# Four graph layers on one core: h rows gathered between the rounds of message sums, the update network's first weight moved into the messages, softplus in one VectorE operation

## The reference

```python
x = _layernorm(x + L0(x, edges, edge_attr_128))     # softmax-weighted messages, 128->256->128 network
x = _layernorm(x + L1(x, edges))                    # sum of neighbours, two matmuls, batch norm, relu
x = _layernorm(x + L2(x, edges, edge_attr_20, edge_weight))
x = _layernorm(x + L3(x, edges))                    # two rounds of mean aggregation
...
# L2: W = filter network of edge_attr_20, times edge_weight; h = x @ W_in2f
# y[n] = sum over edges e with src[e] == n of h[dst[e]] * W[e]
        out = shifted_softplus(y @ W_o1 + b_o1) @ W_o2 + b_o2
```

## Time and profile before

| | |
|---|---|
| three runs | 2384.61, 2387.68, 2387.77 us (median 2387.68) |
| the profiled execution | 2379.15 us, its span 2377.4 us |
| PE busy | 2065.5 us (87%) |
| DVE busy | 1998.6 us (84%) |
| ACT busy | 1792.7 us (75%) |
| POOL busy | 1510.3 us (64%) |
| DMA | mean 182 GB/s |
| mean granted TensorE clock | 0.952 of full speed |

### The profile page before, as it was taken

The page is one execution under the profiler, slowest core; times in us unless marked ns, Lnnn a source line. Parts: engine busy times, 40 slices in busy tenths (PEclk is TensorE's granted clock), DMA queues, the critical chain, the costliest instruction groups (busy, mean ns, idle before and its releaser), DMA issues. The chain is left out here.

```text
span 2377.4 us, 45798 instructions
## 1 busy us (share of the span) xinstructions
PE 2065.5 (87%) x14016; PEld 1722.5 (72%) x14016; DVE 1998.6 (84%) x2960; ACT 1792.7 (75%) x3691; POOL 1510.3 (64%) x1115
## 2 busy tenths in 40 slices
PE   5999999999998899997998788884899995777774
PEld 4999999999997577775776677773666663666663
DVE  7999999999997566666998799993888885788886
ACT  4889899988997577776776688884899994555563
POOL 6888866777730544433555564677888874888774
PEclk9999999999999899998999899997999998789897
DMA  4767666556665888887885687884576764998763
GB/s 111 159 158 161 157 171 169 164 160 192 190 183 180 213 253 252 255 254 176 215 202 127 150 186 179 193 195 124 151 198 186 200 185 118 198 220 215 195 189 113
DMA packets 326072, 433.55 MB, mean 182 GB/s; under 512 B 114207, under 2 KB 170113, under 8 KB 325832
## 3 DMA queue, kind: packets, MB, share of 16 engines
q1 hardware_dynamic: 213528, 373.35, 56.0%
q0 software_dynamic: 112000, 56.93, 14.1%
q10 hardware_dynamic: 304, 0.36, 0.1%
HBM read 242.31 MB, written 188.97 MB: 181 GB/s over the span
## 5 line engine op out<-in xcount | busy, mean ns | idle before, releaser
L1785 POOL DMA_INDIRECT acc<-combined,first_ x100 | 211.4, 2114 | 172.0 <-DMA acc<-combined,first_ 115.8
L511 PE MATMUL banks<-mats,g_hT 128*125 128x256 f32 x1000 | 259.3, 382 | 0.0
L530 PE MATMUL banks<-mats,g_zT 128*125 128x128 f32 x2000 | 238.8, 273 | 0.0
L845 POOL DMA_INDIRECT gin_xs<-x,from_ x100 | 127.9, 1279 | 158.1 <-DMA x_of_src<-gin_xs 134.1
L530 PEld LDWEIGHTS banks<-mats,g_zT 128*125 128x125 f32 x2000 | 228.2, 188 | 0.0
L511 PEld LDWEIGHTS banks<-mats,g_hT 128*125 128x125 f32 x1000 | 189.8, 190 | 28.4 <-issue 0.4
L1013 DVE TENSOR_TENSOR gin_acc<-gin_acc,gin_qr 125x512 f32<-125x512 f32 x125 | 86.6, 693 | 116.5 <-ACT gin_qr L975 116.5
L591 ACT ACTIVATE g_zT<-banks,cols 128x500 f32<-128x500 f32 x250 | 179.1, 776 | 2.6 <-PE banks L519 2.6
L574 ACT ACTIVATE g_sq<-banks 125x512 f32<-125x512 f32 x250 | 144.8, 590 | 43.4 <-PE banks L511 43.0
L438 POOL DMA_INDIRECT g_xd<-in_x,idx x100 | 124.8, 1248 | 70.6 <-PE banks L545 43.7
L2305 POOL DMA_INDIRECT out<-el_h,to_d x100 | 130.8, 1308 | 60.7 <-issue 32.5
(11 more groups left out here) (412 smaller groups left out, 6599.1 us busy)
## 6 DMA issues: line engine op xcount, KB each, us to landing
acc<-g_zero SPq DMA_DIRECT2D x126, 224.0 KB
x<-g_x SPq DMA_DIRECT2D x125, 224.0 KB
g_x<-in_xT SPq DMA_DIRECT2D x100, 250.0 KB
gin_x<-x SPq DMA_DIRECT2D x50, 448.0 KB
h<-gin_hr SPq DMA_DIRECT2D x50, 448.0 KB
al_h<-h SPq DMA_DIRECT2D x32, 448.0 KB
al_x<-x SPq DMA_DIRECT2D x32, 448.0 KB
out<-al_out SPq DMA_DIRECT2D x32, 448.0 KB
```

Source lines behind the costliest of these rows:

```text
L511: m = nc.tensor.matmul(bank[0:P, 256 * j:256 * j + 256], HT[q % 2][:, c:c + P], K.W1c, start=False, stop=j == 1)
L530: m = nc.tensor.matmul(pO[q % 2][0:P, D * j:D * j + D], ZT[q % 2][:, h, P * j:P * j + P], K.W2[:, h, :], start=False, stop=j == R - 1 and ...
L1785: pool.indirect_dma_start(out=K.acc, out_offset=bass.IndirectOffsetOnAxis(ap=K.first[:, g, r:r + 1], axis=0), in_=CR[:, g, r * D:r * D + D ...
```

## The change

Four edits:

1. **h rows.** POOL no longer gathers h rows at the start of the messages and in `edges_middle`. Instead `get_h(k)` follows each of the 25 rounds of sums, in both stages. Tile k of the h rows goes into the tile of `combined` whose sum has just landed (tile 0 into a spare one).
2. **y rows.** Eight tiles (SPARE) are gathered at the end of `side` instead of 20, into spare tiles and tile 0 of `combined`. The other 17 are gathered in `edges_middle`, `get(k)` taking tile k + 8 once tile k of h has been turned. `put` is four tiles late instead of five.
3. **W_o1 in the messages.** `turn_m` multiplies by W_o1 instead of the identity. Since the sum over edges and the multiplication by W_o1 can be exchanged, `acc` holds y @ W_o1, and `first`, `first_d`, `copy_y`, `copy_yd` leave `edges_middle`. ACT and DVE now read the turned y in PSUM directly (pG for the source side, pT for the destination side).
4. **Softplus.** max(v, -b) + ln(1 + exp(-|v + b|)) in one `scalar_tensor_tensor`. The missing constant b - log 2 passes through W_o2 into `bias_u`. For that `Fold` gets three more small DVE operations on constants, one more matmul and one more addition, and `split_rows` (eight DVE operations in iterations 4 to 8 of the messages) makes `bias_u`. `Deferred` no longer makes it in the first layer.

The lists of `steps` for ACT and DVE in `edges_middle` are written in a new order (not shown), the last part of PE's too.

```diff
-YEARLY = 20
+SPARE = 8
...
-        elif n in (4, 5):
-            wide = (K.bias_s if n == 4 else K.bias_u)[:, :].rearrange("p (r d) -> p r d", r=R)
-            part = [p[:, D * (n - 4):D * (n - 3)].rearrange("p (o d) -> p o d", o=1).to_broadcast([128, R, D]) for p in part]
+        elif n == 4:
+            wide = K.bias_s[:, :].rearrange("p (r d) -> p r d", r=R)
+            part = [p[:, 0:D].rearrange("p (o d) -> p o d", o=1).to_broadcast([128, R, D]) for p in part]
...
+        link(nc.vector.tensor_scalar(c[8], K.c("bo1"), LOG2, None, ALU.subtract))
+        link(nc.vector.tensor_scalar(self.passed[:, :], K.ident[:, :], 0.0, c[8], ALU.mult, ALU.add))
+        link(nc.vector.tensor_scalar(c[9], K.c("bo1"), -1.0, None, ALU.mult))
+        dve.wait_ge(self.pc, 2)
         link(nc.vector.tensor_tensor(K.alone[:, :], self.pa[:, 0:128], K.bo2_rows[:, :], ALU.add))
+        link(nc.vector.tensor_tensor(self.rows[:, :], self.pa[:, 128:256], K.bo2_rows[:, :], ALU.add))
...
+    def split_rows(self, dve, n):
+        nc, K, rows, rest, part = self.nc, self.K, self.rows, self.rest, self.part
+
+        def link(ins, count):
+            ins.then_inc(self.split, 1)
+            dve.wait_ge(self.split, count)
+
+        if n == 0:
+            link(nc.vector.tensor_copy(part[0][:, :], rows[:, :]), 1)
+            link(nc.vector.tensor_tensor(rest[:, :], rows[:, :], part[0][:, :], ALU.subtract), 2)
+            link(nc.vector.tensor_copy(part[1][:, :], rest[:, :]), 3)
+        elif n == 1:
+            link(nc.vector.tensor_tensor(rows[:, :], rest[:, :], part[1][:, :], ALU.subtract), 4)
+            link(nc.vector.tensor_copy(part[2][:, :], rows[:, :]), 5)
+        elif n in (2, 3, 4):
+            wide = K.bias_u[:, :].rearrange("p (r d) -> p r d", r=R)
+            piece = part[n - 2][:, :].rearrange("p (o d) -> p o d", o=1).to_broadcast([128, R, D])
+            if n == 2:
+                link(nc.vector.tensor_scalar(wide, piece, K.ident[:, 0:1], None, ALU.mult), 6)
+            else:
+                link(nc.vector.scalar_tensor_tensor(out=wide, in0=piece, scalar=K.ident[:, n - 2:n - 1], in1=wide, op0=ALU.mult,
+                                                    op1=ALU.add), n + 4)
...
+        pe.wait_ge(self.made, 14)
+        nc.tensor.matmul(self.pa[:, 128:256], self.passed[:, :], K.W("o2"), start=True, stop=True).then_inc(self.pc, 1)
...
-                for k in range(4):
-                    ins.get(pool, k)
                 for k in range(rounds):
                     past(pool, cr, k)
                     past(pool, fi, k)
                     past(pool, added, k - 1, 16 * R)
                     sum_round(pool, K, CR, last - k, added)
+                    ins.get_h(pool, k)
                 past(pool, added, rounds - 1, 16 * R)
...
                 def turn_m(k):
                     if k == 0:
-                        pe.wait_ge(bn.made, 13)
+                        pe.wait_ge(bn.made, 17)
                     past(pe, mt, k)
                     past(pe, mr, k - 1)
                     for j in range(R):
-                        m = nc.tensor.transpose(pM[0:P, D * j:D * j + D], MT[k % 2][:, P * j:P * j + P], K.ident[:, :])
+                        m = nc.tensor.matmul(pM[0:P, D * j:D * j + D], MT[k % 2][:, P * j:P * j + P], K.W("o1"), start=True, stop=True)
...
-                steps(EG, [(1, only_last), (2, indices_of), (1, apply), (1, select), (1, weights), (0, residual), (1, sums),
+                steps(EG, [(1, only_last), (2, indices_of), (4, lambda k: bn.split_rows(dve, k)), (1, apply), (1, select), (1, weights), (0, residual), (1, sums),
...
     def side(pool):
         for i, k in enumerate(range(rounds, EG)):
             past(pool, added, i - 1, 16 * R)
             sum_round(pool, K, CR, EG - 1 - k, added)
+            ins.get_h(pool, k)
         past(pool, added, EG - rounds - 1, 16 * R)
-        for m in range(YEARLY):
-            ins.get_y(pool, m, got)
-        pool.wait_ge(got, 16 * R * YEARLY)
+        for m in range(SPARE):
+            ins.get_y(pool, m)
+        pool.wait_ge(ins.h_got, 16 * R * EG)
+        for m in range(SPARE):
+            pool.wait_ge(ins.y_got[m], 16 * R)
...
+    def sums(self, g):
+        return self.CR[:, g, :].rearrange("p (r d) -> p r d", r=R)
+
+    def H(self, k):
+
+        return self.spare[0] if k == 0 else self.sums(EG - k)
+
+    def Y(self, m):
+
+        if m >= SPARE:
+            return self.H(m - SPARE)
+        return self.spare[m + 1] if m + 1 < SPARE else self.sums(0)
...
                 def get(k):
-                    if k >= 4:
-                        past(pool, hT, k - 4)
-                        ins.get(pool, k)
+                    if k + SPARE < EG:
+                        past(pool, hT, k)
+                        ins.get_y(pool, k + SPARE)
...
-                for k in range(YEARLY, EG):
-                    ins.get_y(pool, k, ins.y_late[k - YEARLY])
-                steps(EG, [(0, get), (5, put)])
+                steps(EG, [(0, get), (4, put)])
...
-                steps(EG, [(0, load), (0, load_d), (2, keep_h), (2, keep_x3d), (2, keep_hd)])
+                steps(EG, [(0, load), (0, load_d), (2, keep_h), (2, keep_x3d), (3, keep_hd)])
...
-                    past_slot(pe, got, k, 16 * R)
-                    past(pe, ydt, k - 1)
+                    past(pe, spd, k - 1)
...
                 def turn_y(k):
-                    past(pe, bt, k)
-                    if k >= YEARLY:
-                        pe.wait_ge(ins.y_late[k - YEARLY], 16 * R)
+                    past(pe, sp_, k - 1)
+                    pe.wait_ge(ins.y_got[k], 16 * R)
                     for j in range(R):
-                        m = nc.tensor.transpose(pT[:, P * j:P * j + P], ins.Y(k)[:, j, :], K.ident[0:P, 0:P])
+                        m = nc.tensor.transpose(pG[:, P * j:P * j + P], ins.Y(k)[:, j, :], K.ident[0:P, 0:P])
                     m.then_inc(yT, 1)
 
                 def turn_yd(k):
                     past_slot(pe, din, k, 80)
-                    past(pe, yt, k)
+                    past(pe, bt, k)
...
-                def first(k):
-                    past(pe, yt, k)
-                    past(pe, rld, k - 1)
-                    past(pe, abd, k - 1)
-                    nc.tensor.matmul(pG[:, 0:G], K.W("o1"), YT[k % 2][:, :], start=True, stop=True).then_inc(o1, 1)
-
-                def first_d(k):
-                    past(pe, ydt, k)
-                    past(pe, rl, k)
-                    past(pe, ab, k)
-                    nc.tensor.matmul(pG[:, 0:G], K.W("o1"), YTD[k % 2][:, :], start=True, stop=True).then_inc(o1d, 1)
...
-                steps(EG, [(0, turn), (0, turn_y), (0, turn_back), (1, turn_x3), (0, first), (0, turn_yd), (1, hidden), (1, turn_x3d),
-                           (0, first_d), (1, back_h), (1, second), (0, update), (1, hidden_d), (0, update_d), (1, back_hd)])
+                steps(EG, [(0, turn), (0, turn_y), (2, back_hd), (1, turn_x3), (0, turn_back), (0, turn_yd), (1, hidden), (1, turn_x3d),
+                           (0, update), (1, second), (1, back_h), (1, hidden_d), (0, update_d)])
...
-                def copy_y(k):
+                def size(k):
                     past(act, yT, k)
-                    past(act, o1, k - 2)
-                    nc.scalar.activation(YT[k % 2][:, :], pT[:, 0:G], ACT.Copy).then_inc(yt, 1)
-
-                def copy_yd(k):
-                    past(act, ydT, k)
-                    past(act, o1d, k - 2)
-                    nc.scalar.activation(YTD[k % 2][:, :], pT[:, 0:G], ACT.Copy).then_inc(ydt, 1)
-
-                def size(k):
-                    past(act, o1, k)
...
-                def positive(k):
-                    past(dve, ab, k)
+                def soft(k):
+                    past(dve, l1, k)
                     past(dve, upd, k - 2)
-                    nc.vector.tensor_scalar(SP[k % 2][:, :], pG[:, 0:G], K.c("bo1"), 0.0, ALU.add, ALU.max).then_inc(rl, 1)
-
-                def soft(k):
-                    past(dve, rl, k)
-                    past(dve, l1, k)
-                    nc.vector.scalar_tensor_tensor(out=SP[k % 2][:, :], in0=SP[k % 2][:, :], scalar=LOG2, in1=AB[k % 2][:, :],
-                                                   op0=ALU.subtract, op1=ALU.add).then_inc(sp_, 1)
-
-                def positive_d(k):
-                    past(dve, abd, k)
+                    nc.vector.scalar_tensor_tensor(out=SP[k % 2][:, :], in0=pG[:, 0:G], scalar=floor, in1=AB[k % 2][:, :],
+                                                   op0=ALU.max, op1=ALU.add).then_inc(sp_, 1)
+
+                def soft_d(k):
+                    past(dve, l1d, k)
                     past(dve, updd, k - 2)
-                    nc.vector.tensor_scalar(SPD[k % 2][:, :], pG[:, 0:G], K.c("bo1"), 0.0, ALU.add, ALU.max).then_inc(rld, 1)
-
-                def soft_d(k):
-                    past(dve, rld, k)
-                    past(dve, l1d, k)
```

(34 more changed lines are left out.)

49 lines of the change are left out of this document (23 added, 26 removed).

## The result

The change makes the kernel faster by 0.6%: the ratio is 0.9942, 95% interval 0.9927 to 0.9956, and the medians of 20 runs each are 2386.51 us before and 2374.74 us after (their own quotient, 0.9951, lies inside). Forecast were 2369.4 us and a chance of 0.74 for this side.

A forecast was written before the change was run, and what follows sets the result against it. PE was taken to bound the messages, POOL's `get_y` nodes alone; in edges middle ACT, PE, DVE and POOL were nearly full. Terms -1.9 + 10.5 - 14 - 12.9 = -18.3 from 2387.68 gave 2369.4 us, range 2350 to 2393.

The forecast's parts named there:

- First layer, -1.9: First layer: DVE loses 1.9 us of work on `bias_u`, with work queued behind it; the other bound is 0.
- Messages, +10.5 forecast: Messages: PE's added work and POOL's gathers give the same end, stage 10.5 us longer, +7 to +14.
- `split_rows`, taken as 0: Messages: its added DVE work fits into DVE's free time and PE's delay, costing 0, at most +3.6 us.
- -0.5 was taken: Start of the messages: one more constant matmul, +1.0 us, against -1.5 for h gathers leaving the start.
- a round grows by 0 to 0.7 us: Messages: four h gathers, 6.3 us, fit into POOL's landing wait, 6.5 us on average, so rounds hardly grow.
- 1312.7 at worst: Messages: latest trace time for POOL's last four gathers to end, against engines ending at 1303 + 10.3.
- Nodes alone, -14 forecast: Nodes alone: with fewer `get_y`, SP's last store ends the stage, 14 us sooner, between -11.5 and -16.7.
- the 6 I had added: End of nodes alone: 4 us for the last store's landing plus 2 us for the barrier.
- Edges middle, -12.9 forecast: Edges middle: engines speed up, but POOL's puts waiting for landings, 10.2 us apart, end the stage, saving 12.9 us.
- the M + 308: Edges middle: engines through 308 us after M, the stage's first ACT instruction; puts trail by some 30 us.
- The rival on the slower side: Edges middle: 13 puts without gathers between wait for landings; pitch from 11.7 us makes the sum positive, 2394.6 at 12.3; chance 0.12.
- The first rival: Edges middle: puts keep up at a pitch of 8.4 us, saving 21.6 us more, time 2342 to 2348; chance 0.10.

The follow-up runs named there:

- e5: The change itself, unaltered, as control on its chip; ratio 0.9947 to the kernel before.
- e6: The change with SP's store of h rows one iteration later, so x is loaded earlier; ratio 0.9958 to the kernel before.
- e7: The change with x loads early and three y gathers behind each of puts 0 to 15; ratio 0.9893 to the kernel before.
- e8: The change with turn_m's multiplication by W_o1 put back to the transposition, W_o1 left out of the computation; ratio 0.9953 to the kernel before.
- e11: The kernel before with only the moved gathers of h and y, with 4 spare tiles instead of 8; ratio 1.0041 to the kernel before.
- e12: The change without the moved gathers: W_o1, softplus and new lists, h and 20 y tiles gathered as in the kernel before; ratio 1.0011 to the kernel before.
- e4: The change with 10 instead of 11 rounds of sums in the messages, 15 instead of 14 in nodes alone; ratio 0.9886 to the kernel before.
- e9: The change with ten rounds in the messages, early x loads, y gathers spread between puts and the first put earlier; 2340.78 us, ratio 0.9811 to the kernel before.

## Why the prediction was right, and where it was off

**First layer, -1.9**. Not to be seen: executions differ by 16 us in stages that nobody touched.

**Messages, +10.5 forecast, +15.8 measured (+14.8 in e5, +18.4 and +19.0 in e6 and e7): the term that was mis-sized.** The engines ended the stage's work 200.7 us after its start before and 211.4 after, +10.7 where +10.3 was the sum. That agreement is partly luck. `turn_m` cost what it was to cost, 25 x 0.44 = 11.0 us. But `split_rows`, taken as 0, was not covered. PE's iterations that go with it:

```profile
1176.76 0.59 PE L1621 MATMUL banks<-ident,ef_h 125*128 125x125 f32 x4
...
1178.23 0.74 DVE L1135 SCALAR_TENSOR_TENSOR bias_u<-bn_part,ident,bias_u 128x512 bf16<-128x512 bf16 x1
...
1185.02 0.59 PE L1621 MATMUL banks<-ident,ef_h 125*128 125x125 f32 x4
```

That is 8.26 us; the five iterations with `split_rows` take 7.87 to 8.32 and all later ones 7.70, together +2.4 us. e8 has `split_rows` and the transposition, and its five take 7.56 to 8.00 against 7.26; before and e11, without `split_rows`, have no such iterations. The rest, -2.7 us where -0.5 was taken, is the start of the stage: PE's two waits for loads in the earlier trace rows have gone in this execution. They don't always go: in e6 and e7, with the same messages, PE still waits 1.7 and 1.1 us for an x tile there, and the engines end at 214.0 and 214.6, as in e12 (214.5), where the gathers of h stand at the start again. So the relief at the start is not shown to come from the moved gathers.

POOL, not PE, set the end of the stage. The step that failed was "a round grows by 0 to 0.7 us". The first rounds of the stage started 1132.7 and 1288.7 (ten pitches, 15.6 us each) before, and 1146.9 and 1315.8 (16.9) after: +1.3 each, 13 us over ten. The gathers took 1358 ns, not the 1284 of the earlier trace rows, and four of them with their gaps, 6.6 us, outlast the landing of a round, about 6.0 (15.6 less 9.6). I had taken the mean wait, 6.5 us, from the seven that the profile puts down to a landing; there are ten between eleven rounds, and the other three were shorter. "1312.7 at worst" was 212.2 us after the start; POOL was done at 214.5, and its last landing and the barrier, 3.9 us, were left out. e8 and e4 show both: without the added PE work the stage is as long, with one round less it is 4 to 5 us shorter.

**Nodes alone, -14 forecast, -14.6 measured.** POOL's last gather ended at 1629.8, 295 us into the stage and not 277, which cost nothing, and SP's last store was followed by the next stage:

```profile
1666.13 0.43 SPq L94 DMA_DIRECT2D out<-al_out  x1
```

From its end to ACT's first instruction of the next stage it was 3.5 us, not the 6 I had added; in return the store came 2.0 us later in the stage than before.

**Edges middle, -12.9 forecast, -17.6 measured.** The mechanism was right in each step: POOL slower than the engines in the mixed stretch, a row of puts that wait for landings, engines idle for some 35 us behind them. Put 12 started at M + 211.2 (213 forecast), the pitch was 10.03 (10.2), the last issue ended at M + 337.2 (341.3). DVE, from whose end the M + 308 was counted, was through at M + 302.6, which cost nothing. The rival on the slower side had the right place but too high a price: its pitch of 11.7 was never reached as a mean. The first rival did not come true: a pitch like its 8.4 appeared only in the last three puts (8.5 us), when the engines had stopped. Up to put 21 the pitch was 10.5, so the mean of 10.03 is a mixture, and it falls with every put that is left behind the engines' end.

The Trainium skill, page "DMA: Bandwidth & Descriptors", section "Anatomy of one DMA — SWDGE (gpsimd) path", gives 2.0 us plus bytes / 436e3. By that rule the landing of a put is estimated at 2.15 us. The trace does not agree for indirect puts in traffic: the nine waits that began while the engines worked were 3.0 to 5.9 us, 4.5 on average. The three behind them, 2.7 to 3.0 us, come nearer to it. The measurement decides.

**The sum.** -16.4 us in the touched stages, and -16.4 for the same three terms of the forecast, by two errors of 5 us that cancel. The interval of the ratio is -10.5 to -17.4 us; it holds the -16.4, but not the -18.3 with the first layer in it. A single profile has an uncertainty of some us in each stage (340.0 and 342.7 us for the same edges middle, 217.4 to 221.6 for the same messages), and of the kernel before there is only one, so the rest of the 5.3 us between forecast and median has no term that it could be laid to.

## What to carry to other kernels

When a queue alternates between two kinds of transfers, one of which has to wait for its own landing, spread the others evenly between them: the same 168 DMAs, in a better order and started earlier, were worth some 25 us here (340.0 to 315.3, single executions on two chips, early loads included), and the wait itself could stay. Work moved to "where the queue waits anyway" has to be compared with the wait it fills, instruction by instruction, and what follows the last one counts too. And two edits can be worth nothing apart and 0.6% together, when one lowers the engines' limit and the other the queue's.

## What was not expected of the hardware

The gathers and puts of POOL in edges middle are mostly 1.2 us long, but some take 2.0. After the change 17 of 168 took over 1.9 us, and all 17 overlap DVE's scan (L2207 in e7); of 134 below 1.3 us 4 do, and of 17 between 1.4 and 1.7 us 2. In e7:

```profile
1729.39 1.25 DVE L2207 TENSOR_TENSOR_SCAN em_sum<-same,em_sum,em_x3T 128x500 f32<-128x500 bf16 x1
```

The gather shown above that started at 1729.62 took 2.03 us instead of 1.23, while the f32 operations of DVE beside the two gathers before it left these at their length. That the scan is the cause is argued from the overlap; it was not tried. The Trainium skill, page "DMA: Bandwidth & Descriptors", section "SWDGE vs HWDGE vs iDMA", says that DVE can lock GpSimd out of the descriptor rings in its two-port mode. The overlaps would fit such a lock; no run here shows which mode the scan uses.

The overlap alone does not suffice. In the messages, whose scan reads PSUM, 14 of the 44 gathers of h overlap it, and none of these took over 1.3 us. In e11, 19 of the 22 instructions of edges middle that a scan covers for over a microsecond took 1.4 to 1.5 us. And in e9 this first instruction of a put lies wholly inside a scan and is not longer than others:

```profile
1864.93 1.23 POOL L1938 DMA_INDIRECT out<-combined,first_  x1 [1.66 <-DMA out<-combined,first_]
```

What else it takes stays open.

The other surprise is how close POOL's put with three gathers, one of them long, came to the engines' period in e7, 11.46 us. At such a match a late start of one queue is hardly made up, 3 us in 15 puts here; e9 gained by starting the first put 23 us earlier.
